# Decoder layer on one core: five pairs of self maxima moved into the cross stage, the value-product split put behind the first norm, and a unit-stride ring for cross probabilities

## What is computed

```python
x = _layernorm(x + attn(x, w_qkv, b_qkv, w_proj, b_proj))      # causal, 16 heads of 16
x = _layernorm(x + xattn(x, ctx, ctx, w_q, w_k, w_v, w_o))     # 16 heads of 64, 77 keys
x = _layernorm(x + ffn(x, k0, k1, k2, s0, s1, s2))             # 256 -> 1024 -> 1024 -> 256
```

## Time and profile before

| | |
|---|---|
| median of 3 runs | 2832.47 us (2832.13 to 2832.97) |
| the profiled execution | 2829.64 us, of which its span is 2827.6 us |
| PE busy | 2296.6 us (81%) |
| DVE busy | 1710.5 us (60%) |
| ACT busy | 1150.0 us (41%) |
| POOL busy | 720.4 us (25%) |
| mean granted PE clock | 0.941 of full |
| one pass in the loop | 80.7 us |

### The profile page before, as it was taken

The page is one execution under the profiler, slowest core; times in us unless marked ns, Lnnn a source line. Parts: engine busy times, 40 slices in busy tenths (PEclk is TensorE's granted clock), DMA queues, the critical chain, the costliest instruction groups (busy, mean ns, idle before and its releaser), DMA issues. The chain is left out here.

```text
span 2827.6 us, 54422 instructions
## 1 busy us (share of the span) xinstructions
PE 2296.6 (81%) x18572; PEld 1931.4 (68%) x18572; DVE 1710.5 (60%) x4548; ACT 1150.0 (41%) x2568; POOL 720.4 (25%) x847
## 2 busy tenths in 40 slices
PE   8994688888888788888878788888878788888877
PEld 6883576766676666766667677766667666766666
DVE  4542566666666666666665566666665666666664
ACT  5552344443344334443344334444344334444332
POOL 1000222322322322232232322232232322232231
PEclk9996899999999999999999999999999999999999
DMA  8984322333321332333331232333332232233310
GB/s 265 293 265 95 52 41 51 60 60 60 56 55 46 52 56 34 60 60 60 60 56 48 46 56 34 60 60 60 60 56 47 47 56 38 55 60 60 60 31 12
DMA packets 205155, 196.57 MB, mean 70 GB/s; under 512 B 50130, under 2 KB 184306, under 8 KB 205042
## 3 DMA queue, kind: packets, MB, share of 16 engines
q1 hardware_dynamic: 205108, 195.94, 32.7%
HBM read 69.37 MB, written 58.87 MB: 45 GB/s over the span
## 5 line engine op out<-in xcount | busy, mean ns | idle before, releaser
L1180 PE MATMUL ps<-r_h,w 128*128 128x256 f16 x2048 | 511.6, 289 | 2.1 <-DVE r_l L806 2.0
L1181 PE MATMUL ps<-r_l,w 128*128 128x256 f16 x2048 | 508.9, 288 | 0.0
L821 DVE CUSTOM_DVE_ANT_0 junk<-ps,causal 128x128 bf16<-128x128 f32 (+1 forms) x1024 | 322.8, 353 | 196.5 <-PE ps L1212 188.4
L488 POOL TENSOR_TENSOR p<-p,inv 128x308 f32<-128x308 f32 x256 | 228.4, 899 | 612.1 <-DVE inv L872 612.1
L623 ACT ACTIVATE probs<-ps 128x768 f32<-128x768 f32 x256 | 207.7, 813 | 295.2 <-PE ps L1223 294.4
L598 ACT ACTIVATE p<-ps,low 128x77 f32<-128x77 f32 x1024 | 268.0, 409 | 97.0 <-DVE low L860 94.2
L1318 PE MATMUL ps<-vo_h,p2t 128*128 128x256 f32 (+1 forms) x1280 | 241.9, 291 | 50.9 <-DVE p2t L879 49.2
L475 POOL TENSOR_SCALAR_AFFINE_SELECT probs<-probs 128x512 f32<-128x512 f32 x256 | 164.1, 641 | 430.8 <-ACT probs L623 430.6
L806 DVE SCALAR_TENSOR_TENSOR r_l<-ps,r_h 128x512 f16<-128x512 f32 x256 | 175.7, 687 | 135.8 <-ACT r_h L563 135.7
L1180 PEld LDWEIGHTS ps<-r_h,w 128*128 128x128 f16 x2048 | 211.4, 103 | 55.7 <-issue 20.7
L1223 PE MATMUL ps<-q_st,k_bd 128*128 128x256 f32 x1024 | 180.8, 306 | 74.6 <-DMA q_st<-neg_max 61.0
(11 more groups left out here) (145 smaller groups left out, 5027.3 us busy)
## 6 DMA issues: line engine op xcount, KB each, us to landing
vo_scratch<-vo_out SPq DMA_DIRECT2D x80, 448.0 KB, 4.3
vo<-vo_scratch SPq DMA_DIRECT2D x64, 512.0 KB
q_st<-p2t SPq DMA_DIRECT2D x192, 128.0 KB
k_bd<-p2t SPq DMA_DIRECT2D x192, 128.0 KB, 6.6
q<-q SPq DMA_DIRECT2D x128, 128.0 KB, 2.1
k_bd<-k_scratch SPq DMA_DIRECT2D x64, 154.0 KB, 3.4
x_in<-in_x SPq DMA_DIRECT2D x32, 256.0 KB, 5.4
out<-y SPq DMA_DIRECT2D x32, 256.0 KB, 2.2
```

What stands on the lines that cost most here:

```text
L488: pool.tensor_tensor(heads, heads, inv.unsqueeze(3).to_broadcast([P, TB, 2, SK]), ALU.mult)\
L821: dve.tensor_tensor_reduce(out=junk[:, e, b * P:b * P + width], in0=ps[:, bank + b, e * width:(e + 1) * width], in1=causal[:, (1 - b) * P: ...
L1180: pe.matmul(dst, w1[:, kk, m * P:(m + 1) * P], r0_h[:, kk, :], start=kk == 0, stop=False)
L1181: last = pe.matmul(dst, w1[:, kk, m * P:(m + 1) * P], r0_l[:, kk, :], start=False, stop=kk == KF - 1)
```

## The change

Four edits are made, and no arithmetic is left out.

1. POOL waits for `d_x1` (DVE has normalised `x1`) ahead of splitting `vo`, and does `biased(i + 1)` ahead of the second norm's inverse deviation. DVE normalises `y3` of g (`ffn_norm`) ahead of the residual of `x1`, no longer behind it; SP's store of g waits for that and so is issued earlier.
2. `scores_by_query` and `self_max` always use banks 2 and 3, and each pair waits for all maxima of the pair ahead of it. Pair 0 goes ahead of the transposes of `x1`, with the waits for `q_stacked` and `k_stacked`; pairs 1 to 4 go into the cross stage; pairs 5 and 6 stay behind it. The cross output moves into bank 6 alone, the transposed probabilities into banks 1 and 7, the transposed `x1` into bank 4, the first half of the transposed maxima into bank 7.
3. ACT writes exponentials into a ring of four tiles `p2r` of unit stride; DVE sums there, POOL reads there and writes `p2`. From unit 4 on `cross_exp` waits for POOL's product of unit t-4.
4. Small moves: quarters of layer 1 go from the cross stage to behind it; on ACT `negated_max(i, 1)` goes one exponential earlier, and so does `transposed_x2`; `residual` and one `relu` go among the `cross_probs` of group 1.

```diff
@@ gpsimd
                 inverse_deviation(0, i)
+                pool.wait_ge(d_x1, nth(i, 2, 2))
                 for n, (rows, n0, n1) in enumerate(VO_CHUNKS):
...
-                    heads = unit_probs(t)
+                    raw = p2r[:, t % 4].rearrange("p (b e) k -> p b e k", b=TB)
...
+                if more:
+                    biased(i + 1)
                 inverse_deviation(1, i)
-                if more:
-                    biased(i + 1)
@@ scalar
                 act.wait_ge(d_m2, nth(i, KX, t + 1))
-                heads = unit_probs(t)
+                if t >= 4:
+                    act.wait_ge(g_p2, nth(i, KX, t - 3))
@@ vector
                     self_values(i + 1)
+                if g is not None:
+                    ffn_norm(g)
...
+                if more:
+                    self_max(i + 1, 0)
                 if not first:
                     relu_low(1, r1_h, r1_l, a_r1, d_r1, f, 1)
-                if g is not None:
-                    ffn_norm(g)
...
-                    if t == 4 and more:
-                        self_max(i + 1, 1)
+                    if t in (2, 4) and more:
+                        self_max(i + 1, 1 + t // 2)
@@ tensor, scores_by_query
-                if n == 1:
-                    pe.wait_ge(d_mx, nth(i, 2 * H, 4))
-                if n == 3 and after_cross:
-                    pe.wait_ge(d_y2, nth(i, 1, 0))
-                if n == 2 and not after_cross:
-                    pe.wait_ge(d_mx, nth(i, 2 * H, 8))
-                if n >= 4:
-                    pe.wait_ge(d_mx, nth(i, 2 * H, 4 * n if n == 7 else 4 * (n - 1)))
+                if n >= 1:
+                    pe.wait_ge(d_mx, nth(i, 2 * H, 4 * n))
@@ tensor, attention
                 layer1_until(f, Z_PJ, Z_LN)
+                if more:
+                    pe.wait_ge(q_stacked, nth(i + 1, 112, 112))
+                    pe.wait_ge(k_stacked, nth(i + 1, 96, 96))
+                    scores_by_query(i + 1, 0)
                 pe.wait_ge(d_x1, nth(i, 2, 2))
-                transposes(x1, 3, i, pe_x1t)
+                transposes(x1, 4, i, pe_x1t)
```

More of the change, by code:

```diff
@@ L635, in attention @@
             def attention(i, first, f, first_f=False, more=True):
-                for n in range(4):
+                for n in range(3):
                     self_probs(i, n)
                 negated_max(i, 1)
-                self_probs(i, 4)
+                self_probs(i, 3)
                 if not first:
                     transposed_x2(f)
+                self_probs(i, 4)
                 self_probs(i, 5)
@@ L684, in attention @@
                 cross_probs(i, 0, 1)
+                cross_exp(i, 7)
                 cross_probs(i, 0, 2)
-                cross_exp(i, 7)
-                for c in range(3):
-                    cross_probs(i, 1, c)
                 if not first:
                     residual(f, first_f)
+                cross_probs(i, 1, 0)
+                cross_probs(i, 1, 1)
+                if not first:
                     relu(0, r1_h, pe_z1, a_r1, f, 2)
+                cross_probs(i, 1, 2)
                 if more:
@@ L947, in attention @@
                 cross_probs_low(i, 0, 2)
-                for c in range(3):
-                    cross_probs_low(i, 1, c)
                 if more:
-                    self_max(i + 1, 2)
+                    self_max(i + 1, 4)
+                cross_probs_low(i, 1, 0)
+                cross_probs_low(i, 1, 1)
+                if not first:
+                    relu_low(0, r1_h, r1_l, a_r1, d_r1, f, 2)
+                cross_probs_low(i, 1, 2)
                 if not first:
@@ L960, in attention @@
                 if more:
-                    self_max(i + 1, 4)
+                    self_max(i + 1, 5)
                 layer_norm_apply(1, x2, x2, d_x2, i)
-                if not first:
-                    relu_low(0, r1_h, r1_l, a_r1, d_r1, f, 2)
-                if more:
-                    self_max(i + 1, 5)
                 if not first:
@@ L1261, in transposed_max @@
                 pe.wait_ge(d_mx, nth(j, 2 * H, H * (half + 1)))
-                dst = (ps[0:H // 2, 5, S:2 * S], ps[0:H // 2, 2, 0:S])[half]
+                dst = ps[0:H // 2, (7, 2)[half], 0:S]
                 for b in range(TB):
@@ L1286, in cross_scores, with cross_transposes @@
                 last.then_inc(pe_s2, 1)
-            def cross_transposes(i, g, c, more=True):
+            def cross_transposes(i, g, c):
                 unit = 3 * g + c
@@ L1292, in cross_transposes @@
                     pe.wait_ge(g_p2, nth(i, KX, 4 * g + 4))
-                if unit == 0 and more:
-                    pe.wait_ge(d_mx, nth(i + 1, 2 * H, 8))
                 if unit >= 2:
@@ L1301, in cross_transposes @@
                         probs_in = p2[:, b, g].rearrange("p t h -> p (t h)")[:, n * P:n * P + rows]
-                        last = pe.transpose(ps[0:rows, 2 + unit % 2, (n % 2) * S + b * P:(n % 2) * S + (b + 1) * P],
+                        last = pe.transpose(ps[0:rows, p2t_bank(g, c), (n % 2) * S + b * P:(n % 2) * S + (b + 1) * P],
                                             probs_in, ident[:])
@@ L1317, in cross_output @@
                         for b in range(TB):
-                            last = pe.matmul(ps[:, 6 + b, 0:D], p[0:rows, at, b * P:(b + 1) * P], w[0:rows, at, :],
-                                             start=g == 0 and n == 0 and k == 0, stop=g == 1 and n == VT - 1 and k == 2)
+                            last = pe.matmul(ps[:, 6, b * D:(b + 1) * D], p[0:rows, at, b * P:(b + 1) * P], w[0:rows, at, :],
+                                             start=g == 0 and n == 0 and k == 0 and b == 0,
+                                             stop=g == 1 and n == VT - 1 and k == 2 and b == TB - 1)
                 if g == 1 and c == 2:
@@ L1344, in attention @@
                 scores_by_key(i, 0)
-                if f is not None:
-                    pe.wait_ge(d_mx, nth(i, 2 * H, 24))
                 scores_by_key(i, 1)
@@ L1406, in attention, with next_scores @@
                     pe.wait_ge(d_v, nth(i + 1, 1, 1))
+                def next_scores(n):
+                    if more:
+                        scores_by_query(i + 1, n)
                 cross_queries(i, 0)
+                next_scores(1)
                 cross_queries(i, 1)
@@ L1484, in _ @@
             for n in range(NP):
[L1485 removed]
+                scores_by_query(0, n)
             transposed_max(0, 0)
```

86 lines of the change are left out of this document (34 added, 52 removed).

## The result

The changed kernel takes **2592.72 us** (median of four runs, 2590.38 to 2595.12). The kernel before, run beside it, takes 2832.3 us. The ratio is 0.916, with a 95% interval of 0.9142 to 0.9177. The forecast was 2595 us, range 2500 to 2690. The profiled execution took 2591.91 us; its mean granted clock (PE's clock as a share of full speed) is 0.943, against 0.941 before. Little of the gain is the clock's: in passes 5 to 28 of the two traces PE works 5.7 us a pass at half clock before and 3.9 after, 1.8 us less, of which half, 0.9 us of a pass's 7.5, is saved.

A forecast was written before the change was run, and what follows sets the result against it. PE, busy 81% of the span, was taken as the bound, its gain coming from its waits. -7.6 us a pass over 31 passes (-235.6), -7.9 in pass 31 and +6 in the preamble took 2832.5 to 2595 us, range 2500 to 2690.

The forecast's parts named there:

- C: Stretch from the cross stage's output to the first self scores by key: waits for residual and maxima go, -6.0 us.
- A: Stretch from the end of quarter 12 of layer 1 to the first cross scores: wait and slow clock stay, +1.3 us.
- B: The cross stage: less PE work (-0.5 us) and stalls of 3.65 us where 4.1 were, -1.0 us.
- D: Stretch from the first to the fifth self scores by key: shorter wait for the negated maxima's DMA, -1.1 us.
- E: Stretch from the fifth self scores by key to the first layer 0: the wait for `x2t_l` goes, -1.0 us.
- F: Stretch from the first layer 0 to the end of quarter 12: values 3 may meet POOL early, +0.2 us.
- late next is the wait that edit 2 puts ahead of the transposes: In A: `x1` comes 5.2 us earlier, but PE then waits for the head stacks, landing at 1564.1.
- The rival in which the stacks don't bind: A loses its 5.2 us wait and 2.7 of half clock, 241 us more, 2355 us; chance 0.08.
- looks like a fixed cost: Exponentials in B: ACT issues one every 0.262 us for 77 columns, held against a gain from unit stride.
- the rival in which it pays more: B's stalls fall to 2 us or less through unit stride, about 2540 us; chance 0.17.
- The rival in which the maxima sit on the loop: B's stalls reach 8 us or half clock enters B: +3 to +4.4 a pass, 2690 to 2730; chance 0.22.
- The ends of the run: Preamble's four more full waits for maxima +6 us; pass 31 gains the norm's 5.2 and 2.7 of half clock, -7.9.

## Why the prediction was right

The stretches in us. The last two columns set the changed kernel against the pass of before that has no half clock in C (78.6 us, cut in the same way).

| | before | forecast | after | forecast term | term against the usual pass |
|---|---|---|---|---|---|
| A | 12.6 | 13.9 | 13.1 | +1.3 | +1.4 (11.7) |
| B | 26.5 | 25.5 | 25.2 | -1.0 | -1.3 (26.5) |
| C | 10.3 | 4.3 | 4.4 | -6.0 | -5.1 (9.55) |
| D | 9.7 | 8.6 | 8.4 | -1.1 | -0.9 (9.4) |
| E | 3.0 | 2.0 | 1.9 | -1.0 | -1.1 (3.0) |
| F | 18.6 | 18.8 | 18.5 | +0.2 | 0 (18.5) |
| whole | 80.7 | 73.1 | 71.6 | -7.6 | -7.0 (78.6) |

**A, "late next is the wait that edit 2 puts ahead of the transposes": right**, and the forecast stands on it. PE waits 5.85 us at the pair of self scores, released by the DMA into `k_bd`, with the half clock behind it, as foretold. The last landing is 7.4 us behind its issue (taken: 7.1, from a quick pass), so the stacks come not 0.3 but some 0.7 us behind `x1`: PE waits 5.9 us a pass for them, and waited 5.2 for `x1`. The rival in which the stacks don't bind was priced at 2355 us, the norm's part at 241; that line alone gives 219 in the kernel before, and the kernel in which PE asks for the stacks late enough takes 2374.5. So its price was near, though these are other kernels, and only its condition was not met.

**B: right in sum, by the loop followed.** Forecast were 1.05, 0.75 and 1.35 us at scores 5, 6 and 7 and 0.5 at the first low part, 3.65 in all:

```profile
1540.63 0.79 PE L1280 MATMUL ps<-k_bd,q 128*128 128x154 f32 x4 [0.64 <-ACT p2r L601]
1542.08 0.76 PE L1280 MATMUL ps<-k_bd,q 128*128 128x154 f32 x4 [0.30 <-ACT p2r L601]
1544.85 0.79 PE L1280 MATMUL ps<-k_bd,q 128*128 128x154 f32 x4 [1.58 <-ACT p2r L601]
...
1554.91 0.48 PE L1312 MATMUL ps<-vo_h,p2t 128*128 128x256 f32 x2 [0.73 <-DVE p2t L883]
```

Three stalls at the places named and one behind them, 3.25 us: the sum is nearly right, the shares less so (scores 6 waits 0.30, scores 7 1.58). The sum over `p2r` was to take 470 ns and takes 457. That the exponential "looks like a fixed cost" held: unit stride takes 16 ns off each, so the rival in which it pays more, which needed 1.05 to fall towards 0.8 us a unit, got 0.97. The rival in which the maxima sit on the loop, or bring the half clock into B, did not come about: B's clock is 1.00.

**C, "nothing ends last but PE": right**, 4.43 us of which PE is busy 4.43. **D and E** are right to 0.2 us: no scores by key wait for long and `x2t_l` is in time. E's reason was ACT's earlier copy of `x2t_h`, and the run with the pairs moved back, which leaves E at 1.93 us, fits it. The run with two pairs moved back shows that C's gain hangs on their place.

**The ends of the run** were not right term by term. Set out by the `x1` transposes, in us saved (the forecast's first term is its +6 for the preamble and +1.3 for A):

| | forecast | measured |
|---|---|---|
| to pass 0 | -7.3 | -7.9 |
| 30 passes, to pass 30 | 228.0 (7.6 each) | 223.1 (7.44 each) |
| to pass 31 (7.6, A's +1.3, which pass 31 does not pay, and the norm's 5.2) | 14.1 | 14.4 |
| to the end | 2.7 | 7.8 |
| whole | 237.5 | 237.4 |

In the preamble six of the seven waits between the pairs take 1.49 to 1.50 us, as at 249.88, and the last 1.77. From pass 31's transposes to the end, 2.7 us of half clock were forecast and 7.8 measured. PE's waits there in the kernel before, and a window of it:

```profile
PE ps L1191 <- DVE r_l L806: 3.9, 2, 2.5
PE ps L1284 <- ACT p L598: 2.1, 2, 1.1
...
PE ps L1318 <- DVE p2t L879: 1.5, 3, 1.1
```

```profile
2788.40:2791.70 3.30, 3.26 (x16) 2.33 (x17) 0.00 (x0) 0.00 (x0) 0.00 (x0) 0.50 0.02 5
```

In the changed kernel these waits sum to 2.8, 0.7 and 0.2 us, and PE never works at half clock there. So besides the norm's, a second half clock of some 3.3 us goes, which I had not priced, nor 3.8 us of waits. The unit stride is not what shortens them: with the ring undone they are 2.8, 0.8 and 0.2. Which of the other moves is, no run here tells.

**What was off.** Two terms were mis-sized, and they cancel: 30 passes gave 4.9 us less than forecast, the end 5.1 us more. That the whole comes within 0.1 us by the traces, and 2.3 by the medians, is luck. So is a part of the 7.6. In the pass taken as the measure A grew by 0.5 us and not by 1.3, though the wait grew by more than forecast, since less of the half clock falls on work (3.9 us a pass, where 5.4 were read for it); and that whole pass shrank by 9.1. But it is not the mean pass: its A and C were 0.9 and 0.8 us longer than the usual pass's, by where the half clock fell. The usual pass gives 7.0, the mean of all 7.54.

## What to carry to other kernels

When an engine waits for one thing, look up when its other inputs land: here the norm and the head stacks came due within some 0.7 us of each other, so the line that freed the norm was worth 219 us in one kernel, 7 in the next and 223 in a third. A wait for something late belongs behind all work that does not need it; moving the wait for the stacks, and the pairs behind it, past the first cross queries and scores took 218 us off. And side work on an in-order engine goes behind the instruction that feeds a bank, not ahead of it (62 us for one set of maxima).

## What the runs showed of the hardware that was not expected

- The half clock follows stalls much shorter than A's: 2.95 us is followed by 0.50, and 1.58 us, behind other small waits, by 0.52 in some passes of one kernel and by 1.00 in others. A wait's price is thus its length and at times the half clock's besides; leaving that out made one expectation too low and one too high.
- The same code takes 78.5 to 80.6 us a pass in one execution of the kernel before: 78.5 to 78.9 where the half clock stands in A alone, 79.7 to 80.6 where a second stretch of it falls in C or D. One pass is a poor measure.
- The last DMAs of the stacks take 6.9 to 7.8 us from issue to landing, median 7.4, before and after, whether or not a store is issued behind them. The prediction's 7.1 came from one pass.
